# A two-part attention and expert layer: sequences split 20 and 12 instead of 16 and 16, row transfers by index spread singly

## What is computed

```python
x = x + recurrence(layernorm(x))            # minGRU-like scan over the sequence
h = layernorm(layernorm(x), ln1)
attn = softmax(q @ k.T / sqrt(8)); x = x_ + (attn @ v) @ Wo
m = layernorm(x, ln2)                       # 8192 tokens x 128
wts, idx = top_k(softmax(m @ Wg), 2); wts = wts / wts.sum()
h1 = gelu(m @ W1[e] + b1[e]); ye = h1 @ W2[e] + b2[e]
out = x + sum(wts * ye[idx])
```

## Time and profile before

| what | us |
|---|---|
| median of 3 runs | 1256.87 |
| lowest, highest | 1249.65, 1257.58 |
| the profiled execution's own time | 1244.62 |
| its span in the trace | 1242.7 |

### The profile page before, as it was taken

The page is one execution under the profiler, slowest core; times in us unless marked ns, Lnnn a source line. Parts: engine busy times, 40 slices in busy tenths (PEclk is TensorE's granted clock), DMA queues, the critical chain, the costliest instruction groups (busy, mean ns, idle before and its releaser), DMA issues.

```text
span 1242.7 us, 27732 instructions
## 1 busy us (share of the span) xinstructions
PE 861.5 (69%) x8942; PEld 523.4 (42%) x8943; DVE 890.2 (72%) x1822; ACT 647.2 (52%) x1305; POOL 438.2 (35%) x531
## 2 busy tenths in 40 slices
PE   2677565778888876488888884578887888888000
PEld 1345443133333336123333333556666666666000
DVE  6788597788888816878888846557767777777722
ACT  3655187277777755057777773254545545554000
POOL 5700396011211215023333334125554064440675
PEclk9999699599999975569999986589999989999555
DMA  6900033211111110011111100023332233332422
GB/s 162 358 1 1 1 116 149 58 53 54 48 53 48 53 31 1 5 37 50 58 47 46 47 20 5 12 70 92 97 90 85 65 91 97 98 92 57 135 76 64
DMA packets 110454, 84.71 MB, mean 68 GB/s; under 512 B 12294, under 2 KB 95882, under 8 KB 110362
## 3 DMA queue, kind: packets, MB, share of 16 engines
q1 hardware_dynamic: 80410, 56.22, 14.7%
q0 software_dynamic: 8192, 16.79, 4.9%
q10 hardware_dynamic: 21760, 10.49, 2.9%
HBM read 41.26 MB, written 41.94 MB: 67 GB/s over the span
## 4 chain that ended last, share of the span: by engine, by line
PE 52%; DVE 21%; issue 9%; POOL 8%; ACT 4%; DMA 2%; another core or an unknown queue 1%; ACTq 1%; DVEq 0%; SPq 0%; POOLq 0%
PE bank L1182 47%; DVE arena L993 9%; POOL Z L633 2%; POOL HT L633 2%; DVE mom L850 2%; POOL xh L456 2%; PE bank L1354 2%; POOL rr L452 2%; DVE arena L929 2%; PE bank L1186 1%; PE bank L1439 1%; PE bank L1361 1%; ACT arena L818 1%; ACT arena L725 1%
## 5 line engine op out<-in xcount | busy, mean ns | idle before, releaser
L993 DVE TENSOR_REDUCE arena<-bank 128x2 f32<-128x512 f32 x512 | 337.1, 688 | 75.3 <-PE bank L1182 73.3
L725 ACT ACTIVATE arena<-bank 128x512 f32<-128x512 f32 x512 | 292.8, 596 | 131.4 <-PE bank L1182 127.2
L1182 PE MATMUL bank<-QK 32*128 32x256 f16 (+1 forms) x2048 | 206.8, 286 | 95.6 <-DVE arena L993 71.3
L594 POOL DMA_INDIRECT expert_in<-HT,idx x128 | 135.6, 1060 | 283.6 <-PE bank L1182 269.0
L1182 PEld LDWEIGHTS bank<-QK 32*128 32x128 f16 (+1 forms) x2048 | 63.8, 93 | 246.5 <-ACT arena L725 183.5
L1182 PE MATMUL bank<-w2h,arena 128*128 x1280 | 144.5, 222 | 32.6 <-issue 23.2
L818 ACT ACTIVATE arena<-bank,b1s 128x256 f32<-128x256 f32 x320 | 125.4, 475 | 54.0 <-PE bank L1182 46.1
L1182 PE MATMUL bank<-arena,VA 128*32 128x256 f32 x2048 | 144.8, 403 | 1.4 <-ACT arena L725 1.4
L1182 PEld LDWEIGHTS bank<-w2h,arena 128*128 128x128 f16 x1280 | 110.9, 97 | 59.7 <-issue 53.9
L1182 PE MATMUL bank<-arena,w1h 128*128 128x256 f16 x640 | 113.6, 279 | 22.8 <-issue 13.0
L1182 PE MATMUL bank<-w2l,arena 128*128 x640 | 123.8, 219 | 0.6 <-issue 0.5
(11 more groups left out here) (147 smaller groups left out, 1398.7 us busy)
## 6 DMA issues: line engine op xcount, KB each, us to landing
QK<-qk_parts SPq DMA_DIRECT2D x96, 128.0 KB, 2.6
expert_in<-arena SPq DMA_DIRECT2D x40, 256.0 KB, 3.5
arena<-expert_in ACTq DMA_DIRECT2D x80, 128.0 KB
expert_out<-arena SPq DMA_DIRECT2D x80, 128.0 KB
qk_parts<-arena SPq DMA_DIRECT2D x16, 512.0 KB, 2.8
X<-x SPq DMA_DIRECT2D x8, 512.0 KB, 5.8
wst<-w SPq DMA_DIRECT2D x16, 256.0 KB, 2.8
out<-arena SPq DMA_DIRECT2D x16, 256.0 KB
```

The source lines that it names most:

```text
L594: pool.indirect_dma_start(xs, bass.IndirectOffsetOnAxis(idx[:, k, n:n + 1], 0), MH[:, n, :], None).then_inc(scattered[n // HN], 16)
L725: nc.scalar.activation(PT[t % 8], bank[2 + t % 2][:, :], ACT.Exp, scale=DH ** -0.5)\
L993: V.tensor_reduce(nmax[n % 2][:, :, 4 * j + g], bank[u % 2][:, :].rearrange("p (q t) -> p q t", q=2), AX.X, ALU.max, negate=True).then_inc ...
L1182: return nc.tensor.matmul(dst, lhsT, rhs, start=start, stop=stop)
```

## The change

Part 0 gets 20 sequences and part 1 gets 12. That makes 40 and 24 tiles, 5 and 3 octets, and 48 and 32 blocks; there are still 80 blocks. POOL's three sets of transfers by index get a wait of their own for each transfer, with thresholds spread evenly over the work of the other part: 80 scatters (before 64) over the 192 score steps of part 1, one each 2.4 steps; 48 scatters (before 64) over the first 36 of 48 blocks; and 80 gathers (before 64) over 30 of the 32 blocks of part 1. The final gathers of part 1 are 48 (before 64) and still without a wait between them.

```diff
-SEQ0 = [0, NB // 2, NB]
+SEQ0 = [0, 5 * NB // 8, NB]
...
             for b in range(2, SEQ0[1]):
                 expand(b)
-                split_weight(b - 2)
+                if b - 2 < 2 * NE:
+                    split_weight(b - 2)
...
-            for b in range(SEQ0[1], NB):
-                if b >= SEQ0[1] + 2:
+            for i in range(2 * HN):
+                step = 16 * SEQ0[1] + i * 16 * (NB - SEQ0[1]) // (2 * HN)
+                pool.wait_ge(st_done, step + 1)
+                scatter(i // 2, i % 2)
+                b = step // 16 + 1
+                if SEQ0[1] + 2 <= b < NB and 16 * SEQ0[1] + (i + 1) * 16 * (NB - SEQ0[1]) // (2 * HN) >= 16 * b:
                     expand(b)
-                for q in range(4):
-                    pool.wait_ge(st_done, 16 * b + 4 * q + 1)
-                    scatter(2 * (b - SEQ0[1]) + q // 2, q % 2)
...
             for n in range(HN, NT):
-                if n % 2 == 0:
-                    pool.wait_ge(down_done, (n - HN) + 1)
                 for k in range(2):
+                    pool.wait_ge(down_done, (2 * (n - HN) + k) * (HBLK - 12) // (2 * (NT - HN)) + 1)
                     scatter(n, k)
...
-                    if part == 0 and n >= 2:
-                        pool.wait_ge(down_done, HBLK + n)
                     done = gat_in[1 + (n - HN) // 4 if part else 0]
                     for k in range(2):
+                        if part == 0:
+                            pool.wait_ge(down_done, HBLK + (2 * n + k) * (NBLK - HBLK - 2) // (2 * HN) + 1)
```

## The result

The changed kernel takes 1267.09 us (median of 20 runs), the kernel before beside it 1253.98 (20 runs). The ratio is 1.0051, with a 95% interval from 1.003 to 1.0073: slower by half a per cent, where 1229 was forecast. The ratio of the two medians is 1.0105, since the comparison leaves disturbed runs out. The profiled execution took 1265.27 us, with a span of 1263.5; against the profiled 1244.62 of before that is 20.7 us more, where the sum of the prediction said 27.8 less. So 48.5 us have to be found between the two profiles (by the medians it is 13.1 + 27.8 = 40.9).

The account below looks back on a forecast made before the run. No stage overlaps the next, so time is their sum, the end bound by part 1's gathers. Terms -20.1 - 5.2 - 1.5 - 2.5 + 1.5 = -27.8 us; 1256.87 - 27.8 = 1229 us, range 1215 to 1242.

Parts of the forecast that it names:

- Terms of nothing: Scores, norm, route, block count and weight splits: no cost; ten score sequences still 134.7 us, each scatter ending before the next.
- the slower rival: Scores of part 1: denser scatters delay SP's transfer of the next sequence's maxima, outweighing 27.8 us from 4.7 us delay; chance 0.03.
- Term 1: End stage: 48 final gathers instead of 64, at 1.254 us each, take 20.1 us off, all of it showing.
- Term 2: Expert blocks with scatters: spread scatters no longer meet ACT's loads, 4.09 us a block instead of 4.25; 5.2 us off.
- spreading brings nothing: Rival, expert blocks: ACT's load is late for some other reason, only terms 1 and 3 remain, time 1235; chance 0.15.
- Term 3: Hand-over between the parts: ACT's wait for the last scatters goes, 1.5 us off.
- Term 4: First gathers in part 1's blocks: no longer overdue, so no run without a gap delays ACT; 2.5 us off.
- Term 5: Part 1's blocks: denser gathers, up to three a block, may meet ACT's loads; 1.5 us added, between nothing and 6.6.

Follow-up runs that it names:

- e1_on_pv: Kernel before, with each of its 64 scatters in part 1's scores released two steps later, by the step of a PV group (PE's products with V): 1283.52 us, ratio 1.0275.
- e1_off_pv: Changed kernel, with the 16 scatters released by a PV step released one step later: 1241.9 us, ratio 0.9922; repeated at 1240.0, ratio 0.9882.
- e1_spread_only: Changed kernel's spreading rule with the old cut of 16 and 16 sequences: 1240.99 us, ratio 0.9911 to the kernel before.
- e3_late_start: e1_off_pv with the gathers of part 0 starting two blocks later, the same program as e2_late_start in another set: 1250.0 us, ratio 0.9967.
- set 2: Second of five sets of runs, each with its own runs of the kernel before, which took 1238.6 us here.
- e1_on_next: Kernel before, with the same 64 scatters as e1_on_pv released three steps later, by the step after the PV group: 1251.87 us, ratio 1.0009.
- e4_hold: e1_off_pv with the 48 final gathers held back until DVE has combined the ten groups of part 0: 1239.84 us, ratio 1.001.
- e5_x_each: e1_off_pv with DVE combining into X group by group and SP storing from X, no wait for a store: 1239.6 us, ratio 0.9892.
- e2_late_start: e1_off_pv with the threshold of each gather of part 0 raised by two blocks, as dense as before: 1218.83 us, ratio 0.9839.
- e2_pace: e1_off_pv with a small GpSimd write behind each of the 48 final gathers to space them: 1222.16 us, ratio 0.9855.
- e2_x_in_place: e1_off_pv with the first half of a group's combination written into X instead of the shared tile: 1220.73 us, ratio 0.986.

## Why the prediction was wrong, point by point

**Terms of nothing, the scores: the step that failed, 28 of the 48.5 us in the profile, 16 to 24 by the runs.** The prediction wrote "ten sequences take 134.7 us with four scatters in each and without any" and took it that scatters cost nothing as long as each ends before the next. Both rows are true, but they show scatters at one place only, released by step 4q, ahead of the PV group. The change moved 16 of 80 to the PV step. `e1_on_pv` shows that the old number of scatters at the new place costs 31 us, `e1_off_pv` that the new number off that place is nearly free. My test "14 us or more would be the slower rival" was tied to the wrong mechanism: sequences did reach 14 to 18.8 us, with the maxima on time in the one shown. Some 5 of the 28 us are not the PV steps: the second sequence of part 1 took 18.2 us here, but 16.3 to 18.9 in nine variants without PV releases too, and 13.5 in the kernel before. Why the clock comes up a sequence later there is not known. The step of 0.842 us, which the prediction used to show that each scatter ends in time, is a mean: a PV step alone takes 1.34 us even before.

**The clock.** The prediction priced a late transfer by its own length. A stretched step costs 0.3 to 0.8 us; a sequence mostly at half clock costs 5.3. That multiplied the loss.

**Term 1, the final gathers: right in size, but its cover was lost.** The 48 gathers of the changed kernel, first and last:

```profile
1187.65 0.95 POOL L634 DMA_INDIRECT Z<-expert_out,idx  x1 [6.56 <-DMA expert_out<-arena]
...
1246.78 0.94 POOL L634 DMA_INDIRECT HT<-expert_out,idx  x1 [0.30 <-issue]
```

That is a spacing of 1.258 us (forecast 1.254), and 16 fewer of them. But the prediction had "What follows the last gather does not change", and here the span ends 16.7 us behind the last start, not 11.2. It had costed DVE's groups of part 0 at 2.47 us each to the tenth. From 1206.95 on DVE's halves start 2.8 to 5.6 us apart, and its waits are for a signal of its own; ten groups instead of eight reach into that time. 5 us of the term went there. In the kernel before DVE had combined part 0 by 1169.52, 17 us after the first final gather.

**Term 2, blocks with scatters: right.** L1143, 39 blocks from the tenth on, in the changed kernel:

```profile
893.80:1052.70 158.90, 16.26 (x40) 1.00 0.26 78
```

4.07 us each (forecast 4.09, before 4.25), and ACT's load leaves 0.2 us behind the transposes. The rival "spreading brings nothing" is out, also by `e1_spread_only`.

**Term 3, the hand-over: right.** ACT has no wait for scatters in the changed kernel's blocks.

**Term 4, the first gathers: wrong.** ACT in the changed kernel at that place:

```profile
1062.09 0.56 ACT L811 ACTIVATE arena<-bank,aff 128x256 f16<-128x256 f32 x1 [5.00 <-remote]
```

5.0 us, as 5.68 before. The step "the first gather waits for the down of block 48, about one block after the store" forgot what else it waits for: the stores have to land. When they had, six gathers were due at once, and ran from 1052.58 on with 1.25 to 1.6 us between their starts. `e3_late_start` took that burst away, and the 5 us wait with it. Both rows show six gathers in a row, where the prediction counted seven. In the changed kernel ACT's load itself left late there, at 1061.65. The Trainium skill, "DMA: Bandwidth & Descriptors", section "SWDGE vs HWDGE vs iDMA", calls transfers issued from ACT immune to interference on the path on which GpSimd's descriptors are built. The prediction took its late load to speak against that. If, as in the scores, it is the signal ahead of the load that comes late, these traces say nothing for or against that sentence.

**Term 5, denser gathers: the mechanism was right, the size was not.** 18 blocks of the changed kernel:

```profile
1078.80:1157.10 78.30, 7.51 (x18) 1.00 0.37 101
```

4.35 us each, 0.28 above 4.07, over 30 blocks 8.4 us; I took 1.5, and my upper bound was 6.6. (In set 2, without lateness, blocks of the same density take 4.04 us and the term is nothing.) That bound charged the price of a hit to the 20 blocks with three gathers. In fact the 21 loads behind the one at 1061.65 leave 0.9 to 2.8 us behind the transposes, so all blocks pay, not only those with three gathers. As I read it, a late load delays the next down, and the gathers that it releases come closer to the load behind; "as each group starts afresh at a down" then was the wrong argument, as the down itself comes late. No run takes that chain apart.

**The range.** 1215 to 1242 rested on one profile in which scatters and loads met in known ways, and gave the scores no term of their own. The one rival on the slow side had 0.03. The parts that I did price come to about half of what I said: `e1_off_pv`, which removes the unpriced one, measures 0.9882 and 0.9922 of before, that is 10 to 15 us faster where 27.8 were forecast; the rest is terms 4 and 5 and the end.

**What stays open.** Why signals are late in some sets and not in others, and whether the changed kernel would then be faster by the 1.5% that its repaired variants show there. Why DVE's own signals turn late some 17 to 24 us into the final gathers in the kernels cut 20 and 12, but with 16 and 16 only in the last two or three groups, and in `e1_on_next` in none; `e4_hold`, meant for it, fell into a set without lateness. What part of the density of gathers is free, if density it is (1.7 a block is, 2.67 is not).

**The best kernels.** With lateness `e5_x_each`, `e1_off_pv` and `e1_spread_only` are alike at 0.988 to 0.992 of before, and each beats the changed kernel (1.0051 to 1.0088) by 1.3 to 2%. Without it `e2_late_start`, `e2_pace` and `e2_x_in_place` stand at 0.984 to 0.986. The edit of `e1_off_pv` is in all of these but `e1_spread_only`, which has no release by a PV step anyway.

## What to carry to other kernels

A row that shows an operation to be free shows it for the place where it stands. Before moving it, list with which step of the other engines its start will coincide that it never met before, not only whether its queue has room; thresholds by a formula such as one in 2.4 steps visit every place. Price a delay on an engine whose clock can fall by the time that the clock costs, not by its own length. And when runs of the reference differ by 1% from one set to the next, put the changed kernel and its variants into the same set, or a variant may be praised for the set that it fell into.

## What the runs showed of the hardware

- Beside GpSimd's transfers by index, signals between engines that have nothing to do with them arrive late: PE's to ACT and DVE alike by 0.3 us with one transfer started at a PV step and 0.8 with two in the changed kernel, and by 0.2 to 0.8 with one in `e1_on_pv`; the load of ACT by up to 5 us, as read from its start alone; DVE's own signal to itself by up to 4.5 us (9.0 in `e5_x_each`). In the changed kernel SP, waiting for the same signal, wakes with DVE: the store leaves at 1251.71 and DVE's next half starts at 1251.79, 4.4 us behind the end of the half that signalled.
- DVE's starts in the late stretch are 3.5, 4.2, 4.9 or 5.6 us apart, all multiples of 0.7, but for one or two at its ends.
- This differs from set to set, with 14 us in the kernel before (1252 and 1238) and up to 31 in a variant (`e3_late_start` 1250.0, `e2_late_start` 1218.83).
- A row of DVE instructions with two SBUF inputs and no wait between them held a gather of GpSimd for 18.86 us, to 0.8 us behind the end of the row; with a wait after every four or eight no gather was held.
- POOL's own pace is not touched by the lateness: 48 and 64 gathers in a row start 1.25 to 1.27 us apart on average in every kernel (1.28 in `e2_pace`), apart from the two held by DVE.
